# Node update of a four-layer graph network: the turn of new rows moved a pair later and ahead of the second product, and half of the input rows added by VectorE

## The reference

```python
h = jnp.maximum(_layernorm(x, axis=-1), 0.0)
x = x + _L2_gnn_ref(h, edge_index, edge_attr_64, L2_gnn_W1, ...)
h = jnp.maximum(_layernorm(x, axis=-1), 0.0)          # input of the fourth layer
...
def _L2_gnn_ref(x, ...):                              # x is h here
    ...
    agg = jax.ops.segment_sum(messages, dst, num_segments=x.shape[0])
    u = mish(jnp.concatenate([x, agg], axis=-1) @ W3 + b3)
    out = u @ W4 + b4
    y = x + out
    mu = jnp.mean(y, axis=-1, keepdims=True)
    var = jnp.mean(jnp.square(y - mu), axis=-1, keepdims=True)
    return (y - mu) * jax.lax.rsqrt(var + LN_EPS) * gamma + beta
```

## Time and profile before

| | us |
|---|---|
| median of 3 runs | 2826.0 (2825.43 to 2830.35) |
| the profiled execution's own time | 2847.13 |
| its span | 2845.4 |
| node update, first product to last `lo` | 1861.5 to 2411.8 of the span |
| TensorE busy over the span | 2446.0 (86%), mean granted clock 0.943 |
| VectorE, ScalarE, GpSimd busy over the span | 1907.5, 1520.3, 1122.4 |

### The profile page before, as it was taken

How to read it: one execution, slowest core, us unless ns; L and a number is a source line. 1 busy time by engine, 2 the same in 40 slices (tenths; PEclk the granted TensorE clock), 3 DMA queues, 4 the chain that set the end, 5 groups by cost and what they waited for, 6 DMA issues and landing times. The chain is left out here.

```text
span 2845.4 us, 45119 instructions
## 1 busy us (share of the span) xinstructions
PE 2446.0 (86%) x13421; PEld 1424.2 (50%) x13421; DVE 1907.5 (67%) x4612; ACT 1520.3 (53%) x2246; POOL 1122.4 (39%) x1908
## 2 busy tenths in 40 slices
PE   1648898799789999898978979989999997998954
PEld 1435564344344455444544537766666664444443
DVE  8838886687568866898863436668888887223343
ACT  7637774354335533454335756668888775232280
POOL 1567744254333322555545511124444444001155
PEclk9669999999999999999988989999999998999976
DMA  5545543488559888666544332233333444001187
GB/s 200 204 139 158 156 143 122 124 202 179 117 131 222 203 150 173 222 220 217 185 157 125 103 95 76 90 105 120 121 118 121 142 142 154 3 6 52 45 289 292
DMA packets 374158, 413.92 MB, mean 145 GB/s; under 512 B 192822, under 2 KB 232037, under 8 KB 371182
## 3 DMA queue, kind: packets, MB, share of 16 engines
q1 hardware_dynamic: 347918, 337.27, 40.2%
q0 software_dynamic: 26080, 74.68, 9.0%
HBM read 172.47 MB, written 198.18 MB: 130 GB/s over the span
## 5 line engine op out<-in xcount | busy, mean ns | idle before, releaser
L215 PE MATMUL s_ps_z<-own_weights,slots 128*128 128x512 f16 x2844 | 638.9, 382 | 7.8 <-PEq L163 7.8
L215 PEld LDWEIGHTS s_ps_z<-own_weights,slots 128*128 128x128 f16 (+1 forms) x2844 | 279.1, 98 | 325.0 <-issue 18.0
L1756 ACT ACTIVATE s_g<-s_g,s_rn 128x512 f32<-128x512 f32 x237 | 169.8, 716 | 226.9 <-POOL s_rn L1615 226.7
L1615 POOL TENSOR_TENSOR s_rn<-s_em,minus_half 128x1 f32<-128x1 f32 x237 | 179.7, 758 | 219.0 <-DVE s_em L1684 211.6
L1665 DVE SCALAR_TENSOR_TENSOR s_g<-s_ps_z,s_f,s_bias 128x512 f32<-128x512 f32 x237 | 177.9, 751 | 103.4 <-PE s_ps_z L215 90.8
L2565 PE MATMUL u_ps_z<-slots,weights 128*128 (+2 forms) x1920 | 215.9, 273 | 4.2 <-PEq L163 4.2
L2701 PE MATMUL z_ps_z<-slots,weights 128*128 128x512 f16 (+1 forms) x960 | 212.3, 381 | 2.4 <-PEq L163 2.4
L2565 PEld LDWEIGHTS u_ps_z<-slots,weights 128*128 128x128 f16 x1920 | 186.4, 98 | 26.9 <-issue 4.4
L2670 DVE BATCH_NORM_STATS2 z_stats<-slots 128x6 f32<-128x512 f32 (+1 forms) x76 | 52.2, 687 | 187.9 <-ACT slots L2687 187.9
L1675 DVE SCALAR_TENSOR_TENSOR s_junk<-s_g 128x512 f32<-128x512 f32 x237 | 164.5, 694 | 4.1
L215 PE MATMUL s_ps_z<-s_wn,s_aT 128*128 128x512 f16 x720 | 165.2, 379 | 1.8 <-DVE s_aT L1498 1.8
(11 more groups left out here) (435 smaller groups left out, 5558.2 us busy)
## 6 DMA issues: line engine op xcount, KB each, us to landing
h_rows<-s_g SPq DMA_DIRECT2D x237, 256.0 KB, 2.7
x_rows<-q_x SPq DMA_DIRECT2D x79, 256.0 KB
s_halves<-x_rows SPq DMA_DIRECT2D x79, 256.0 KB
x_rows<-s_halves SPq DMA_DIRECT2D x79, 256.0 KB
u_x<-x_rows SPq DMA_DIRECT2D x79, 256.0 KB
x_rows<-u_x SPq DMA_DIRECT2D x79, 256.0 KB
h_rows<-u_h SPq DMA_DIRECT2D x79, 256.0 KB
weights<-x_rows SPq DMA_DIRECT2D x79, 256.0 KB
```

Source lines behind the costliest of these rows:

```text
L215: ins = nc.tensor.matmul(out_ap, a(c), w[:, part * size + c * n:part * size + (c + 1) * n], start=first and c == 0 and m == 0, stop=stop a ...
L1615: nc.gpsimd.tensor_tensor(out=self.rn[b][:, :], in0=self.em[b][:, :], in1=minus_half[:, :], op=POW).then_inc(self.s_rn, 1)
L1756: nc.scalar.activation(self.g[b][:, :], self.g[b][:, :], ACT.Relu, scale=self.rn[v.buf(2)][:, 0:1]).then_inc(self.s_h, 1)
```

## The change

Three things are done.

1. `turn`, `hi` and `lo` work on the pair three behind instead of two. On TensorE `turn` now stands right behind `update` and ahead of `second`. On ScalarE `hi` now stands ahead of `hi_u`. On VectorE `lo` keeps its place in the queue.
2. For the even tile of each pair from 0 to 27 (`by_rows`), the 8 products with `unscale` are left out of `second`. SyncE loads the rows from `h_d[3]` into one of two `zg` buffers a step ahead, and VectorE adds them, scaled by `k_b`, to `ps_o` at the head of `centred(0)`.
3. The first two loads of message products into `zg` wait until all 28 such additions are done.

```diff
+    PAIR_LOOP_END = 28
...
+    ROWS_BELOW = 2 * PAIR_LOOP_END
+    def by_rows(v):
+        return v.j % 2 == 0 and not (isinstance(v.t, int) and v.t >= ROWS_BELOW)
...
                         if e >= 2:
                             sp.wait_ge(s_added, added(v.t - 2))
+                        else:
+                            sp.wait_ge(s_rows, ROWS_BELOW // 2)
...
+                def load_rows(v):
+                    if by_rows(v):
+                        b = v.j // 2
+                        wait_count(sp, s_rows, v.g - 1)
+                        sp.dma_start(zg[b][:, :], slot_rows(h_d[3], v.t)).then_inc(rows_in[b], 16)
...
                     of_pair(v, 1, load_x)
+                    of_pair(v, 0, load_rows, (0,))
                     of_pair(v, -1, load_zg)
...
                 def centred(v):
                     dve.wait_ge(s_mm4, v.t + 1)
+                    if by_rows(v):
+                        dve.wait_ge(rows_in[v.j // 2], 16 * (v.uses(4) + 1))
+                        nc.vector.scalar_tensor_tensor(out=ps_o[v.buf(2)][:, :], in0=zg[v.j // 2][:, :], scalar=k_b[:, 0:1],
+                                                       in1=ps_o[v.buf(2)][:, :], op0=MUL, op1=ADD).then_inc(s_rows, 1)
+                        dve.wait_ge(s_rows, v.g + 1)
...
                     of_pair(v, -1, add_messages(1))
-                    of_pair(v, 2, lo)
+                    of_pair(v, 3, lo)
...
                     of_pair(v, 2, next_rows, (1,))
+                    of_pair(v, 3, hi)
                     whole_pair(v, 0, hi_u)
-                    of_pair(v, 2, hi)
...
-                    for part in range(2):
-                        for c in range(C):
-                            nc.tensor.matmul(ps_o[b][:, c * P:(c + 1) * P],
...
+                    if not by_rows(v):
+                        for part in range(2):
+                            for c in range(C):
+                                nc.tensor.matmul(ps_o[b][:, c * P:(c + 1) * P],
...
                     whole_pair(v, 0, update)
+                    of_pair(v, 3, turn)
                     of_pair(v, 1, second)
-                    of_pair(v, 2, turn)
```

## The result

The changed kernel takes 2943.97 us, median of 4 runs (2941.09 to 2946.93), where the kernel before takes 2825.72: ratio 1.0408, 95% interval 1.0393 to 1.0422, 4% slower. The forecast was 2920. The profiled execution took 2941.09.

A forecast was written before the change was run, and what follows sets the result against it. It took a one-step ring of waits through `h4` to bound the node update: 79 us for the ring, 4 for the end and 11 for the clock make 94, so 2826 becomes 2920 us, own range 2895 to 2945.

The forecast's parts named there:

- the two rings: Node update: waits closing through the `h4` buffer, 15.23 us a pair in the loop, and through `ps_t`, 13.96.
- the clock term: TensorE's clock falling behind the new stall before `turn(0)`: 0.3 us a pair, 11 us; bounds 0 to some 2 a pair.
- Step 1: TensorE's 8 products with `unscale` gone in 28 pairs: 0.46 us each, 12.9 us if TensorE stayed the bound.
- Step 2: Row addition on VectorE: 0.80 us, bounds 0.65 to 0.95, fitting by load; row loads and `load_zg`'s wait cost nothing.
- Steps 3 and 4: TensorE's `turn` waits for VectorE's `lo`, ScalarE's `next_rows(0)` for `turn`: 2.20 us more a pair, 79 us over 36 steps.
- The `h4` ring: One-step chain `lo`, `turn`, `next_rows(0)`, ScalarE's queue, `hi_u`, `residual(0)`, `lo`: 15.23 us in the loop, 16.65 in the zone.
- The other ring: Chain from `lo` freeing `ps_t` through `turn`, `second` and VectorE back to `lo`: 13.96 us in the loop, 15.65 in the zone.
- The cover of 1.3 us: Path through `second(0)` and VectorE's row addition to `hi_u` lies off the ring's path, with 1.3 us over.
- The end: After the last pair, one more pass through `turn`, `hi` and `lo` stands alone: 4 us, bounds 2 to 6.
- TensorE the bound, with the gain arriving: Rival: `lo` ends before `update`, so neither `turn` nor `next_rows(0)` waits, and TensorE's saving arrives: 2813 us, chance 0.03.
- Only the `ps_t` ring: Rival: `next_rows(0)` doesn't wait; 0.93 us more a pair in the loop, 1.2 in the zone: 2866 us, chance 0.08.
- The clock low in every pair: Rival: low TensorE clock costs 2.3 us a pair through `second(0)`, 83 us more over 36 steps: 2992 us, chance 0.04.

The follow-up runs named there:

- the turn alone: Against the changed kernel, all rows again come in by products on TensorE, the moved `turn` kept: ratio 1.0365 to the kernel before.
- the stall filled: Against the changed kernel, nine products with overwritten result put on TensorE between `update` and `turn`: ratio 1.0305 to the kernel before.
- `add_beta` first as well: Against the changed kernel, nine idle products on TensorE before `turn`, and GpSimd's `add_beta` ahead of `y_factor(0)`: ratio 1.0316 to the kernel before.
- the rows alone: Against the changed kernel, `turn`, `hi` and `lo` back at lag 2 in their old places, row addition kept: ratio 1.0007 to the kernel before.
- both rings opened: Changed kernel with `lo` earlier and `next_rows(0)` behind `tanh` in steps 0 to 27, then old order at lag 3; `add_beta` ahead of `y_factor(0)`: ratio 1.0266.

## Why the prediction was right, and where it was off

The two waits and the two rings are right; the surplus of 24 us over the forecast comes in the main from the size of the clock term. The measured 2944 lies only 1 under the upper end of the range, 2945 (the lower end stands as 2895 in one place and as 2885 in another). And of what the prediction said would make it wrong, one came: the granted clock of the stage is 0.91. The term it belongs to has 1.0 a pair as its upper case, which is why the range held.

- **Step 1, the products.** Right that their 12.9 us don't show while the ring is longer: at full clock the loop is 15.31, the ring's. Even without the turn only 0.14 a pair arrives.
- **Step 2, the addition.** 0.76 where 0.80 was taken. No wait for `load_rows` or of `load_zg` is among the long waits.
- **Steps 3 and 4, the waits.** Both are in the table of waits. The `h4` ring, measured with the clock kept, is 15.31 and 16.54 for 15.23 and 16.65. The other ring is 14.11, and 15.63 in most zone pairs, for 13.96 and 15.65. The stall before `turn(0)` is 2.0 in the mean for 2.4.
- **The cover of 1.3 us** for the addition and `second(0)`. It was right at full clock: another 0.70 costs nothing. At the low clock it is used up in the loop: `turn` to the addition grows by 6.06 - 4.48 = 1.58, and then `lo_u` meets `add_beta` and adds 0.8. Together that is 1.1 more than the cover, as in the step shown (16.44 for 15.31). So the row addition isn't free in the changed kernel: 16.21 with it, 15.46 with the turn alone. The collision I had not seen at all: the cover was computed with `lo_u` at its length in the trace of before.
- **The clock, the mis-sized term.** 0.3 a pair, 11 us, was taken. Measured is 16.21 - 15.31 = 0.90 in the loop and 0.51 in the zone, 30 us in the stage. That lies in the bounds of 0 to 2, but the value taken came from too rare a fall: in the loop the clock is low in three steps of every four (last section), and each such step also has the collision; in the zone it is low in every step. This is 19 of the 21 us by which the stage grew beyond the 94. In the zone the 0.51 is near the 0.43 that the prediction gave for a low clock at `turn(0)`.
- **The end.** 10.5 for 4, beyond the bounds of 2 to 6. It is 7.1 with the stall filled and 5.7 with `add_beta` first as well, so part of it is the clock's and the collision's. Which of its parts takes the rest is open.
- **The rivals.** TensorE the bound, with the gain arriving: undone by the rows alone, 1.0007, and by both rings opened, 13.09 in the loop, so a TensorE that is 100% busy gives back at most 0.14 of 0.46, since the chain through `next_rows` is nearly as long. The Trainium skill, "Perfetto Trace Analysis", section "Identifying the Most-Contended Engine", says to optimise the engine with the highest occupancy first, but that the busy share of TensorE's matmuls is no good measure of how near it is to its limit; it names the share of peak arithmetic and the busy share of the weight loads as the good ones. In the window of the earlier trace rows the weight loads are busy 119.87 of 176 us, 0.68, and ScalarE 0.83. So by the weight loads TensorE is not the fullest engine, and that only 0.14 of 0.46 came back agrees with it. The point from which that rival decides was too near: with `lo` 1.7 earlier the period is still 13.84. Only the `ps_t` ring: in this kernel the `h4` ring is the longer at full clock and in the zone, and the two are equal at the low clock in the loop. The clock low in every pair: this came true in the zone and nearly in the loop, but the price of 2.3 took `turn(0)` and all of `second(0)` as low, 3.65 more. Measured are 1.58 more, as the clock is back before `second(0)` ends.

The periods in fours are one step at full clock and without the collision, three with both. Open is why just every fourth keeps its clock. More buffers for `h4`, which might open its ring without another order, were not tried.

## What to carry to other kernels

When a step is moved to another pair, write down for each buffer which instance of the writer now waits for which instance of the reader, and count the steps around; a ring that closes in one step puts everything queued behind its waits into the period, however idle the engines look. A busy share of 100% doesn't say that less work gives less time: look at the second longest chain first. And price a new stall of the product engine by what its clock does to the next leg of the same ring, and by whom the later engine will then meet.

## What the hardware showed that was not expected

- **A VectorE operation with two SBUF inputs waits out one of GpSimd's.** In the kernel after `add_beta` runs from 2066.59 to 2069.09, and `lo_u`, started at 2068.07, takes 2.24 for its two halves, where it takes 1.41 with GpSimd idle. The same view, over 2066 to 2069 us, has the first half alone:

```profile
2068.07 1.58 DVE L2462 SCALAR_TENSOR_TENSOR u_lo<-u_uT,u_g,u_hi 128x512 f16<-128x512 f32 x1
```

  That is 1.58 for about 0.75, and it ends at 2069.65, 0.56 after `add_beta`. `times_z`, with one input in PSUM, runs beside `add_beta` from 2066.59 on and takes its usual 1.65. The Trainium skill, "SBUF — State Buffer", section "SBUF: two separate sides", says that VectorE, in an operation with two SBUF inputs, and GpSimd hold a shared pair of ports exclusively for a whole instruction and that the other is fully blocked. The trace agrees but for the start: an operation that was blocked in full would end 0.75 after `add_beta` and not 0.56, and the `lo_u` of the earlier trace rows, which starts 0.26 before its `add_beta` ends (2052.41 + 2.50), loses only some 0.06 (1.47 for 1.41). Moving `add_beta` shortens the period (16.21 to 15.63, 13.15 to 12.89).
- **In the loop the clock fell in three steps of four, at stalls that look alike.** Timeline of TensorE after, transposes and the eight `u_hi` products of tile 0, four steps in a row:

```profile
2042.42 1.25 PE L226 MATMUL u_ps_t<-ident,u_h 128*128 128x128 f32 x8 [1.81 <-DVE slots L2499]
2043.92 1.90 PE L2614 MATMUL u_ps_o<-weights,u_hi 128*128 128x512 f16 x8
...
2060.00 2.81 PE L2614 MATMUL u_ps_o<-weights,u_hi 128*128 128x512 f16 x8
...
2074.19 1.25 PE L226 MATMUL u_ps_t<-ident,u_h 128*128 128x128 f32 x8 [1.82 <-DVE slots L2499]
2075.81 3.43 PE L2614 MATMUL u_ps_o<-weights,u_hi 128*128 128x512 f16 x8
...
2090.73 1.31 PE L226 MATMUL u_ps_t<-ident,u_h 128*128 128x128 f32 x8 [1.93 <-DVE slots L2499]
2092.30 3.34 PE L2614 MATMUL u_ps_o<-weights,u_hi 128*128 128x512 f16 x8
```

  1.90 is the time at 2.4 GHz, 3.62 that at 1.2 (with both rings opened, at 2340.28); so 2.81 has about half of the eight at 1.2, and 3.43 and 3.34 have most. Behind 1.81 us of idle time the clock stayed, behind 1.82 it fell, and behind 2.37 it was low from the first transposes on. Further on it is the other way round: it stayed behind 1.82 (at 2107.26) and fell behind 1.81 (at 2139.02). So the length of the one stall doesn't tell it. In all three steps it was back for tile 1. Nine idle products took the window's clock from 0.92 to 1.00, and the kernel from 1.0408 to 1.0305.
